# Local attention in a fused Macaron network: scores of even and odd heads issued in turn, two groups at a time

## What is computed

```python
HEADS, DIM_HEAD, WINDOW, DEPTH = 8, 64, 64, 2
def local_attention(q, k, v):                 # after l2norm and rotary
    bq = q.reshape(b, h, w, WINDOW, d) * 8.0
    bk, bv = look_around(bk), look_around(bv) # this window's keys and those of the one before
    sim = jnp.einsum('bhwid,bhwjd->bhwij', bq, bk)
    mask = (i < j) | (i > j + WINDOW) | (j == -1)
    sim = jnp.where(mask, -jnp.finfo(sim.dtype).max, sim)
    attn = jax.nn.softmax(sim, axis=-1)
    return jnp.einsum('bhwij,bhwjd->bhwid', attn, bv)
x = x + 0.5 * _L0_ffn_ref(_layernorm(x), ...)   # first block
x = x + _L0_attn_ref(_layernorm(x), ...)
x = x + 0.5 * _L0_ffn_ref(_layernorm(x), ...)   # third block
x = x + 0.5 * _L1_ffn_ref(...); x = x + _L1_attn_ref(...); x = x + 0.5 * _L1_ffn_ref(...)
```

## Time and profile before

| | |
|---|---|
| median of 3 runs | 5217.1 us (5216.88 to 5219.88) |
| the profiled execution | 5220.88 us, span of its instructions 5219.0 us |
| PE busy | 4264.2 us, 82% of the span |
| PEld / DVE / ACT / POOL busy | 49% / 60% / 53% / 40% |
| mean granted TensorE clock | 0.899 of full speed |
| score products L1365 | 2048 matmul records, 411.8 us busy |

### The profile page before, as it was taken

The page is one execution under the profiler, slowest core; times in us unless marked ns, Lnnn a source line. Parts: engine busy times, 40 slices in busy tenths (PEclk is TensorE's granted clock), DMA queues, the critical chain, the costliest instruction groups (busy, mean ns, idle before and its releaser), DMA issues. The chain is left out here.

```text
span 5219.0 us, 54771 instructions
## 1 busy us (share of the span) xinstructions
PE 4264.2 (82%) x16866; PEld 2561.9 (49%) x16866; DVE 3123.1 (60%) x5606; ACT 2750.7 (53%) x6089; POOL 2092.8 (40%) x1576
## 2 busy tenths in 40 slices
PE   6878897888878798697977979779897788878866
PEld 4446554555445464464644646346454455545522
DVE  4346557556576565765657656666557656476465
ACT  4456556455565455554555545645456455565432
POOL 3003335334264342542434434444345344264344
PEclk9889899898998899898998989989899898998877
DMA  3020013011131111211121111211113011031122
GB/s 95 1 81 1 30 39 113 28 43 42 32 106 40 31 46 61 73 44 34 49 76 55 49 32 49 91 38 51 32 39 113 26 45 36 31 113 34 50 76 74
DMA packets 188859, 274.31 MB, mean 53 GB/s; under 512 B 23449, under 2 KB 102901, under 8 KB 188533
## 3 DMA queue, kind: packets, MB, share of 16 engines
q1 hardware_dynamic: 167652, 234.89, 14.3%
q10 hardware_dynamic: 20880, 35.52, 2.3%
HBM read 215.54 MB, written 54.79 MB: 52 GB/s over the span
## 5 line engine op out<-in xcount | busy, mean ns | idle before, releaser
L586 POOL TENSOR_TENSOR work<-work 128x512 f32<-128x512 f32 x512 | 657.9, 1288 | 1143.2 <-DVE work L646 1079.1
L1340 POOL TENSOR_TENSOR work<-work,minus_half 128x8 f32<-128x8 f32 x256 | 467.8, 1841 | 682.0 <-DVE work L1323 680.4
L646 DVE SCALAR_TENSOR_TENSOR work<-work,psum 128x512 f32<-128x512 f32 x528 | 361.6, 685 | 430.8 <-ACT work L578 430.7
L578 ACT ACTIVATE work<-psum 128x512 f32<-128x512 f32 x528 | 315.1, 597 | 574.8 <-PE psum L554 564.2
L554 PE MATMUL psum<-work,w_up 128*128 128x512 f32 x1024 | 549.6, 620 | 70.2 <-DVE work L646 64.0
L560 PE MATMUL psum<-work,w_down 128*128 128x512 f32 x1024 | 540.8, 610 | 10.8 <-POOL work L586 10.8
L1271 PE MATMUL psum<-wqkv,xn 128*128 128x512 f32 x768 | 434.2, 700 | 82.3 <-DVE xn L1564 80.2
L1440 ACT ACTIVATE work<-psum,work 128x128 f32<-128x128 f32 (+1 forms) x1024 | 392.3, 398 | 157.8 <-DVE work L1460 157.3
L1404 PEld LDWEIGHTS psum<-work 128*128 128x128 f32 x3072 | 376.9, 191 | 71.3 <-issue 52.4
L1365 PE MATMUL psum<-work 64*128 64x128 f32 (+1 forms) x2048 | 411.8, 336 | 0.0
L1404 PE MATMUL psum<-work 128*128 128x64 f32 x3072 | 405.1, 275 | 0.0
(11 more groups left out here) (211 smaller groups left out, 8966.1 us busy)
## 6 DMA issues: line engine op xcount, KB each, us to landing
work<-expert_weight_rows SPq DMA_DIRECT2D x1024, 128.0 KB, 2.9
position_scores<-work SPq DMA_DIRECT2D x64, 768.0 KB, 3.5
work<-position_scores SPq DMA_DIRECT2D x64, 512.0 KB, 3.8
work<-state_readout_rows ACTq DMA_DIRECT2D x72, 256.0 KB, 3.8
cent<-state_readout_rows ACTq DMA_DIRECT2D x32, 256.0 KB, 3.7
sq<-state_readout_rows ACTq DMA_DIRECT2D x24, 256.0 KB, 3.6
rows<-in_L_attn_q SPq DMA_DIRECT2D x8, 256.0 KB, 3.5
expert_weight_rows<-work SPq DMA_DIRECT2D x16, 128.0 KB, 2.3
```

Of the source, the lines that this page charges most:

```text
L578: nc.scalar.activation(self.tanh_h[p % self.turns][0:rows], bank(b, self.ups[p % self.turns])[0:rows], ACT.Tanh, scale=0.5).then_inc(self. ...
L586: pool.tensor_tensor(h, h, self.weights[p % self.SLOTS], ALU.mult).then_inc(self.gated, 1)
L646: v.scalar_tensor_tensor(out=self.gate_h[p % 3][0:rows], in0=self.tanh_h[p % self.turns][0:rows], scalar=1.0, in1=bank(b, self.ups[p % sel ...
L1340: pool.tensor_tensor(half, half, b.minus_half[:].broadcast_to([128, LH]), ALU.pow).then_inc(self.inv_norm, 1)
```

## The change

The scores of groups `m` and `m`+1 are now issued together by one function, for `m` = 0, 2 and 4: both masks first, then the heads of both in turn (even head to one bank, odd head to the other), so that each product's rows of the array differ from those of its neighbour. The wait for the banks is for `exped` of both groups before. Groups 2 and 3 are issued in round 2, groups 4 and 5 in round 4 (before: 2, 3, 4 and 5 in rounds 1, 2, 3 and 4). DVE takes the two maxima of a pair in the same round. In rounds 2 and 4 ACT does `copy_probs` ahead of `exps`.

```diff
-    def group_scores(self, pe, i, m):
+    def pair_scores(self, pe, i, m):
...
         if 6 * i + m >= 2:
-            pe.wait_ge(self.exped, 6 * i + m - 1)
-        out = self.scores(m)
+            pe.wait_ge(self.exped, 6 * i + m)
         mask = b.mask_bf[:, 0:128] if t == 0 else b.mask_bf[:, 128:320]
-        nc.tensor.matmul(out, b.ident_bf[:], mask.unsqueeze(1).broadcast_to([128, len(heads), n]), start=True, stop=False)
+        for side in range(2):
+            nc.tensor.matmul(self.scores(m + side), b.ident_bf[:], mask.unsqueeze(1).broadcast_to([128, len(heads), n]), start=True, stop=False)
         for x, head in enumerate(heads):
-            rows = slice(64 * (head % 2), 64 * (head % 2) + 64)
-            ins = nc.tensor.matmul(out[:, x], self.q_t[i % 2][rows, head // 2, t * 128:(t + 1) * 128],
-                                   self.k_t[i % 2][rows, head // 2, keys:keys + n], start=False, stop=x == len(heads) - 1)
-        ins.then_inc(self.s_ready, 1)
+            for side in range(2):
+                rows = slice(64 * side, 64 * side + 64)
+                ins = nc.tensor.matmul(self.scores(m + side)[:, x], self.q_t[i % 2][rows, head // 2, t * 128:(t + 1) * 128],
+                                       self.k_t[i % 2][rows, head // 2, keys:keys + n], start=False, stop=x == len(heads) - 1)
+                if x == len(heads) - 1:
+                    ins.then_inc(self.s_ready, 1)
...
         if r == 0:
-            self.group_scores(pe, i, 0)
-            self.group_scores(pe, i, 1)
+            self.pair_scores(pe, i, 0)
...
-            if m + 2 < self.GROUPS:
-                self.group_scores(pe, i, m + 2)
+            if m in (1, 3):
+                self.pair_scores(pe, i, m + 1)
...
-            if m + 1 < self.GROUPS:
+            if m in (0, 2, 4):
                 self.exps(act, i, m + 1)
             if i % 2 == 0:
                 self.copy_probs(act, self.nc.scalar.copy, i, m)
+            if m in (1, 3):
+                self.exps(act, i, m + 1)
...
-            if m + 2 < self.GROUPS:
+            if m in (1, 3):
+                self.maxima(dve, i, m + 1)
                 self.maxima(dve, i, m + 2)
```

## The result

The changed kernel takes 5160.6 us (5153.4 to 5165.0 in 4 runs) against 5218.5 for the kernel before on the same chip: ratio 0.9888, 95% interval 0.9871 to 0.9905. It is faster by 1.1%, 58 us; forecast were 5152 and a range from 5105 to 5255.

What follows compares the result with a forecast made beforehand. PE bounds odd passes end to end; in even passes PE's savings are mostly lost at DVE. Gains of 1.5 + 1.03 + 0.5 + 1.03 = 4.06 us per block, x 16 = 65 us, gave 5152 us, range 5105 to 5255.

Steps and rivals of the forecast that it cites:

- Lower end: Score pairs, two records streaming at a time: 1.62 us for 128-column groups, 1.26 for 192-column ones; the case taken.
- Upper end: Score pairs, each record waiting for the one before: 2.47 us for 128-column groups, 1.90 for 192-column ones.
- The fixed 0.3 us per group: Score products: time outside streaming for switching between 128-row and 64-row products; three fewer switches save 0.9 us a pass.
- Rival B: Score products: weight loads set the pace, 128-column records gain nothing, 192-column ones a quarter; 5235 us; chance 12%.
- Round 0 of odd passes: Turn of group 0 starts 3.95 us after the first mask instead of 3.80; 0.16 lost, PE waits some 1.3.
- Round 1, 0.25 for the copy of the heads: Odd passes: L1508 needs ACT's copy L1541, which starts behind the exponentials; about 0.25 us wait.
- Round 4, gating wait: Odd passes: group 4's exponentials wait for the pair, Gelu's table load queues behind, gating comes later; about 0.4 us wait.
- Pass 0: First even pass, starting at half clock: a pair costs 2.97 us, 2.1 less; ACT takes some, 1.5 kept.
- The saved time of rounds 1 and 3: Even passes: 1.1 us saved by PE in each round is hidden behind ACT and DVE and counts nothing.
- Pass 2: Second even pass: DVE starts 0.3 us earlier, one maximum (0.5) leaves the stretch ahead of L646; 0.5 gained in all.
- Rival A: Score products: no overlap, record follows record; odd passes +1.7 us, whole 5267 us, slower; chance 20%.
- Its point of decision: Pace of L1365 in rival A: the loss begins when a 128-column record costs over about 0.09 us.

Runs made afterwards that it cites:

- experiments 3 and 5: 3: changed kernel with two single groups in each pair's place, 5242.4 us; 5: changed kernel with groups 0 and 1 single, later pairs kept, 5222.4 us.
- experiment 2: Changed kernel with all score products reading partitions 0 to 63, so pairs are merged without different halves; 5233.0 us, ratio 1.0024 to the kernel before.
- experiment 1: Changed kernel without alternation: in a pair all even-group heads are issued first, then all odd-group heads; 5175.9 us, ratio 0.9919 to the kernel before.

## Why the prediction was right

The time, its sign and its mechanism were right. That the sum came so close is partly luck: the attention passes gave less than forecast, and time that the prediction did not count came in elsewhere.

- **Price of a pair: right.** Lower end 1.62 and 1.26 us; measured 1.62 (1005.55 to 1007.17) and 1.27. Upper end 2.47 and 1.90; measured with the same half 2.50 and 1.91. The fixed 0.3 us per group, an estimate from rows of the trace before, held: merging two groups in the same half saved 0.32 and 0.27. Rival B (weight loads set the pace) is out: the loads of the two halves overlap too, as in the load records at 1006.184 and 1006.190, 0.19 us each. The rule in the Trainium skill, "TensorE: Matmul & The Clock Gate", Part 3, that products in distinct row groups run together, starting about 4 ns apart, holds here with 7 ns.
- **Round 0 of odd passes: right.** Turn of group 0 predicted 3.95 us after the first mask, measured 4.00; wait predicted 1.3, measured 1.29.
- **Round 1, 0.25 for the copy of the heads: didn't come.** L1513 starts at 1010.05 as soon as the turn is over. A wait of 0.33 exists where round 0 doesn't wait, in experiments 3 and 5, and there it ends with DVE's copy of the heads and not with ACT's. With the change that copy is over at 1009.16, ahead of the turn at 1009.55.
- **Round 4, gating wait: mis-sized,** 0.4 predicted, 0.72 measured. Odd pass in all: -1.03 predicted, -0.87 measured.
- **Pass 0: the step that failed.** "I keep 1.5." It measured 0.0 in the third stage, 2.4 in the first and a loss of 1.7 in the blocks alone. The pair itself gave the 2.1 us that was forecast (2.98 against 5.08), and the projections behind it 0.7 more, because the clock rose earlier in the pass: the turn of group 0 comes 5.74 us after the first mask, 8.53 before. The saved time of rounds 1 and 3 was said to be hidden and to count nothing. It was hidden, but it did count: as idle time of PE, behind which the clock fell. The prediction named a lower clock as a sign to look for in odd passes, where PE is dense; it came in even ones, and in two of the four odd passes of the blocks alone.
- **Pass 2:** 0.5 predicted, 0.84 measured in the third stage and 1.75 in the first, a loss of 2.9 alone. In the first stage the gain is partly the clock's (0.95 before, 0.97).
- **The sum.** By the table the attention passes give 5.9 us per first-stage block, 2.5 per third-stage block, and lose 6.2 per block alone (its odd passes lose 0.8 each at clock 0.97): 7 x 5.9 + 7 x 2.5 - 2 x 6.2 = 46 us, where 65 were forecast. The spans differ by 60: 13 us come from between the attention passes, where the change touches nothing. 7 of them lie in the rounds behind pass 1 of the third-stage blocks, 1.0 us each, and are the clock's; sums by window there, before and with the change:

```profile
1031.60:1064.58 32.98, 29.71 (x96) 16.83 (x94) 24.63 (x42) 18.55 (x30) 21.89 (x15) 0.90 0.17 56
1038.07:1070.03 31.96, 27.11 (x95) 15.32 (x94) 24.53 (x42) 18.55 (x30) 21.87 (x15) 1.00 0.17 58
```

  For the prediction this is luck: outside the attention passes the kernel before takes 3122 us, and every version here 3098 to 3110, also those that are slower in all; why, no run shows. Against the kernel before, each version's total holds 12 to 24 us of this kind. The 72 us between experiment 2 and the change do not: their attention passes differ by 74.
- **Rival A was priced too high:** 5267 predicted, 5233 measured without overlap. Its gating wait was taken as 1.0 because group 4 is ready later. But PE, which has to run the longer pair itself, comes to the gated product later too: measured 0.24, from the start of L1528 at 1035.95 back to where it would stand without a wait. In all an odd pass got 0.45 us longer, where 1.7 were priced. A wait has to be counted from where the waiting engine then stands. Its point of decision, a loss from 0.09 us per record on, isn't tested by these runs.

## What to carry over

Products that contract over 64 rows ran side by side when they lay on different halves of the partitions and wrote different banks (both halves on one bank weren't tried): put the halves next to each other, and count the fixed cost of each switch between 64-row and 128-row products (0.3 us a group here). Before merging steps, look at what the second half used to cover; here L1365 of group 1 covered ACT's exponentials of group 0, and a guest's step put into that gap gave 39 us more. Where an engine other than PE holds a stretch, time saved on PE there can be worse than nothing, because the clock can fall behind PE's idle time: leave such stretches as they were, or move work into them. And compare the stretches that a change touches, not the totals alone: a stretch it does not touch can run at another clock.

## What the runs showed of the hardware that I had not expected

- Matmuls don't always start in program order: in experiment 1 the first record of the odd half started at 1004.745 us, ahead of three even-half records issued before it (1004.851 the next). The Trainium skill, "TensorE: Matmul & The Clock Gate", Part 3, says that matmuls start and end in strict program order; here the measurement decides against it for the starts, for products on different row groups and banks (the ends are modelled).
- Adding 0.9 and 1.1 us of useless mask products to PE's waits in each even pass made the program 30 us faster (5160.6 to 5130.3), the clock of pass 0 in the third stage rising from 0.83 to 0.92.
- The same waits don't always bring the clock down: 1.1, 0.6 and 1.4 us in pass 0 did in 7 of 7 third-stage blocks and in 1 of 7 first-stage blocks, and a wait of 1.2 us in pass 2 of the kernel before did in 7 of 7 first-stage blocks and in none of the third stage.
- The blocks without guests, with the same change, lose 1.7 us in pass 0 and 2.9 in pass 2 at clocks of 0.79 and 0.88, where the blocks with guests gain or stay. Their first two waits at the turns of pass 0 are longer, 1.57 and 1.48 us where the blocks with guests have 1.13 and 0.57.
